# Layer 2's state step: GpSimd adds both halves of a step's output in one operation of 1024 columns

## The chip, the cores and the metric

The kernel runs on one core of one Trainium2 chip. The core has five engines that run side by side: TensorE (PE, matrix products, with its weight loads as PEld), VectorE (DVE), ScalarE (ACT), GpSimd (POOL) and SyncE (SP, here mostly an issuer of DMAs). They wait for one another through semaphores. The metric is the time of one execution on the device in microseconds (us), lower is better; the number given is the median of several runs.

## What is computed

Four layers in a row; each is `x = x + s * silu(f)`, with a sequence mixer s and a mixture of experts f, both of the normalised x. The change lies in layer 2, whose mixer is a selective scan over 512 places for four batches, 256 channels and 16 states:

```python
def step(h, inp):
    dt_t, B_t, C_t, x_t = inp
    h = jnp.exp(dt_t[..., None] * A) * h + dt_t[..., None] * B_t[:, None, :] * x_t[..., None]
    y = jnp.einsum('ben,bn->be', h, C_t)
    return (h, y)
...
y = (y + x_main * D_param) * jax.nn.silu(z)
y = jnp.einsum('ble,de->bld', y, W_out)
out = y + residual
```

Its mixture has 8 experts with 512 hidden units each, of which every token takes two. Each is computed for all tokens and weighed.

## The kernel before

Channels lie on the 128 partitions in two halves m, places along the columns, so one tile of a batch is 128 x 2 x 512, that is 1024 columns. The 16 states are taken one after the other. So layer 2 is a loop of 64 steps k (4 batches b, 16 states n), written out by hand for each engine, and the order in which an engine's code stands is the order in which it works. A step k on the engines:

- ScalarE, `decays(k)` (L2270): the decay factors of a state, into `DA` (`wide` in the trace).
- TensorE, `b_row` and `c_row` (L2102, L2108, in the trace L410, banks<-BCR,SEL): spreads B's and C's row of the state over all partitions, into a PSUM bank.
- VectorE, `inputs(k)` (L2423): DTX times B's row, into `H[:, k % 4]`, one of four buffers; `scan(k)` (L2430): the recurrence along the columns, both halves in one operation with decays and inputs as operands, both in SBUF; `outs(k)` (L2438): H times C's row, two operations of 512 columns, each of which counts the semaphore `hc` up by one.
- GpSimd, `add_y(k)` (L1985): adds H to the running sum `YY`, two operations of 512 columns. For the first state of a batch the sum starts from `XD`, the D term.

VectorE's loop is software-pipelined: in step k it issues scan(k), outs(k-1), inputs(k+2) and, in even steps, `add_expert` (L2454), four operations that add an expert's output for the four tiles of tokens. inputs(k+2) overwrites the buffer of step k-2, so it waits until `ya`, which counts GpSimd's adds, says that add_y(k-2) is done. Between these, at set values of n, stand each batch's other parts: the next batch's normalisation (`stats_in`), router (`take_logits`, `choose`, with L2381), step sizes (`correction`, `dt_sums` with L2408, `dt_x`) and the last batch's end (`gated` L2461, which waits for all 32 adds of its batch, `take_out`, `out_stats`, `finish`).

GpSimd's loop is: add_y(k-1), then at n = 2 the norm's `scales` for the next batch (L381, L382, L1964, L1965, small operations), at n = 4 `out_scales` (L381, L382, L1972, L1973), and in the last batch `early_scales` for layer 3. It works through them in order.

TensorE runs the experts between the rows of B and C: `hidden` (banks<-XT,we) and `chunk` (banks<-we,HH), and in steps 4 to 10 of a batch the projections for the next one. c_row(k) waits for both halves of outs(k-1), since there is one bank for C's row.

Of the kernel before, what the change touches and what calls it, by code (L numbers as in the profile page):

```python
# [20 lines left out]
ALU = mybir.AluOpType  # L21
# [12 lines left out]
def build(nc, I, out):  # L34
    ctx = ExitStack()
    with ctx:
# [3 lines left out]
        def sbr(name, shape, dt=F32, c=None):  # L40
            return sb(name, shape, dt, c, "right")
# [4 lines left out]
        def linker(eng, chain):  # L46

            n = [0]

            def link(ins):  # L50
                n[0] += 1
                ins.then_inc(chain, 1)
                eng.wait_ge(chain, n[0])
            return link
# [324 lines left out]
        def norm_pool(plink, var, rs):  # L379

            plink(nc.gpsimd.tensor_scalar(rs, var, EPS, None, ALU.add))  # L381
            return nc.gpsimd.tensor_tensor(rs, rs, neg_half[:, 0:rs.shape[1]], ALU.pow)  # L382
# [32 lines left out]
        def lsem(name):  # L415
            h = scope[0].enter_context(nc.semaphore(name))
            lsems.append(h)
            return h
# [1449 lines left out]
        def layer2(fcT, pjT, feats, wide, XM, mv3, rstd3):  # L1868
# [6 lines left out]
            bm, ex, scn, hc, ya, yi = (lsem(f"a2_{k}") for k in ("inputs", "decays", "scans", "outs", "y", "y_begun"))  # L1875
# [26 lines left out]
            for k in range(NK):  # L1902
                b, n = divmod(k, NS)
# [19 lines left out]
            with ExitStack() as c:  # L1923
                DTX = sbr("DTX", [P, 2, 2, S], c=c)
                H = sbr("H", [P, 4, 2, S], c=c)
                YY = sbr("YY", [P, 2, S], c=c)
# [15 lines left out]
                XD = [SA4[:, 3, :, :].rearrange(flat), SA[:, :, :].rearrange(flat)]  # L1942
# [7 lines left out]
                with nc.Block() as block:  # L1950
                    @block.sync
                    def _(sp):
                        sp.dma_start(wrow, bcast(I["L2_attn_conv_w"].rearrange("e a k -> (e a k)"), 768)).then_inc(wr, 16)

                    @block.gpsimd
                    def _(g):
                        plink = linker(g, pl)

                        def scales(b):
                            g.wait_ge(var, b + 1)  # L1960
                            if b:
                                g.wait_ge(xn, T * b)
                            plink(norm_pool(plink, mv[:, :, 1], rstd[:, :]))
                            plink(nc.gpsimd.tensor_tensor(shift[:, :], mv[:, :, 0], rstd[:, :], ALU.mult))  # L1964
                            nc.gpsimd.tensor_scalar(shift[:, :], shift[:, :], -1.0, None, ALU.mult).then_inc(rs, 1)  # L1965

                        def out_scales(b):
                            g.wait_ge(var2, b + 1)
                            if b:
                                g.wait_ge(xo2, T * b)  # L1970
                            plink(norm_pool(plink, mv2[:, :, 1], rstd2[:, :]))
                            plink(nc.gpsimd.tensor_tensor(shift2[:, :], mv2[:, :, 0], rstd2[:, :], ALU.mult))  # L1972
                            nc.gpsimd.tensor_scalar(shift2[:, :], shift2[:, :], -1.0, None, ALU.mult).then_inc(rs2, 1)  # L1973

                        def add_y(k):
                            b, n = divmod(k, NS)
                            if n == 0 and b:
                                g.wait_ge(yz, b)
                            for m in range(2):
                                if n == 0:  # L1980
                                    g.wait_ge(yi, 2 * b + m + 1)
                                else:
                                    g.wait_ge(ya, 2 * k + m - 1)
                                g.wait_ge(hc, 2 * k + m + 1)
                                nc.gpsimd.tensor_tensor(YY[:, m, :], YY[:, m, :] if n else XD[m], H[:, k % 4, m, :],  # L1985
                                                        ALU.add).then_inc(ya, 1)

                        def early_scales(b):
                            ts = slice(b * T, (b + 1) * T)
                            g.wait_ge(nv, b + 1)  # L1990
                            if b:
                                g.wait_ge(nx, T * b)
                            else:
                                g.wait_ge(xn, T * B)
                            plink(norm_pool(plink, mv3[:, ts, 1], rstd3[:, ts]))
                            plink(nc.gpsimd.tensor_tensor(shift[:, :], mv3[:, ts, 0], rstd3[:, ts], ALU.mult))
                            nc.gpsimd.tensor_scalar(shift[:, :], shift[:, :], -1.0, None, ALU.mult).then_inc(nr, 1)

                        nc.gpsimd.memset(XT[:, :, 0:1], 0.0)
                        nc.gpsimd.memset(XT[:, :, S + 1:S + 2], 0.0).then_inc(zd, 1)  # L2000
                        nc.gpsimd.memset(BCR[0:32, :, :].bitcast(F32), 0.0).then_inc(zd, 1)
                        scales(0)
                        g.wait_ge(wj, 2)
                        nc.gpsimd.memset(DA[:, :, 1, 0:1], 0.0).then_inc(zd, 1)
                        for k in range(1, NK):
                            b, n = divmod(k, NS)
                            add_y(k - 1)
                            if n == 2 and b + 1 < B:
                                scales(b + 1)
                            if n == 4 and b:  # L2010
                                out_scales(b - 1)
                            if b == B - 1 and n in (2, 5, 8):
                                early_scales((2, 5, 8).index(n))
                        add_y(LAST)
                        out_scales(B - 1)

# [1253 lines left out]
```

## Time and profile before

| | |
|---|---|
| median of 3 runs | 1391.28 us (1389.5 to 1394.29) |
| the profiled execution | 1392.78 us, its span 1391.0 us |
| busy: TensorE / its weight loads | 1151.0 (83%) / 811.3 us (58%) |
| busy: VectorE | 999.5 us (72%) |
| busy: ScalarE | 763.7 us (55%) |
| busy: GpSimd | 614.8 us (44%) |
| layer 2's steps | some 758 to 1184 us of the span |

The span runs from the first instruction of the program to the last; the rest of an execution's time lies around it. A row of a timeline gives start, length, engine, line, operation, the tiles that it writes and reads, their shape, and in brackets how long the engine sat idle before it and who ended that; x4 means that four like instructions were merged to one row. Where a line is a helper's (L410 is every product), the tiles tell which it is. The chain of work that ended last, as the page gives it, covers only the last part of the program and says nothing on layer 2; a stage is read by its window.

### The profile page before, as it was taken

The page shows a single profiled execution, that of the slowest core. Times are in us where ns is not written, and L with a number is a line of the kernel's source. Part 1 is how long each engine was busy: PE and PEld are TensorE (multiplying, and loading weights), DVE is VectorE, ACT ScalarE, POOL GpSimd, SP SyncE. Part 2 cuts the span into 40 slices and gives each one's busy share as a digit, 9 for nine tenths or more (in the row PEclk, how much of TensorE's full clock was granted, in tenths as well). Part 3 has the DMA queues.
Part 4 walks back from the last instruction along what each step waited for, and adds up shares of the span by engine and source line. Part 5 has one row for each costly group of instructions (what it writes and reads, how often), then busy time and mean ns, then how long its engine had stood idle before and what let it go on. Part 6 is the DMA issues. An engine that isn't in the chain of part 4 may idle for free. (4 is left out here: it accounts for less than half of the span.)

```text
span 1391.0 us, 21029 instructions
## 1 busy us (share of the span) xinstructions
PE 1151.0 (83%) x7010; PEld 811.3 (58%) x7010; DVE 999.5 (72%) x2280; ACT 763.7 (55%) x1586; POOL 614.8 (44%) x607
## 2 busy tenths in 40 slices
PE   3999999999898879367766888888888977889995
PEld 1455665665465568156653655655645655668885
DVE  2466767678787727277765989989998999535555
ACT  1456556555544527144446867667768675345552
POOL 4243445444336834554100533733643565216672
PEclk9999999999999989589987999999899889799997
DMA  7400000000000023550000000000000000101113
GB/s 176 121 1 1 1 1 1 1 1 1 1 5 22 28 63 116 154 163 16 1 13 0 1 1 1 1 1 1 1 1 1 1 1 0 31 10 40 43 44 107
DMA packets 54443, 40.71 MB, mean 29 GB/s; under 512 B 13185, under 2 KB 46687, under 8 KB 54337
## 3 DMA queue, kind: packets, MB, share of 16 engines
q1 hardware_dynamic: 40994, 27.58, 6.8%
q0 software_dynamic: 4544, 9.32, 2.4%
q10 hardware_dynamic: 8800, 2.48, 0.9%
q8 instruction: 58, 0.95, 0.3%
q14 instruction: 47, 0.39, 0.1%
HBM read 26.32 MB, written 13.04 MB: 28 GB/s over the span
## 5 line engine op out<-in xcount | busy, mean ns | idle before, releaser
L780 POOL TENSOR_TENSOR PR<-PR,R 128x512 f32<-128x512 f32 (+3 forms) x128 | 160.3, 1264 | 233.1 <-DVE R L1275 232.5
L1985 POOL TENSOR_TENSOR YY<-YY,H 128x512 f32<-128x512 f32 x120 | 164.1, 1390 | 182.0 <-DVE H L2438 182.0
L410 PE MATMUL banks<-XT,we 128*128 128x128 f32 (+1 forms) x568 | 175.8, 442 | 14.0 <-ACT HH L2258 13.7
L1074 ACT ACTIVATE PR<-banks,NM 128x257 f32<-128x257 f32 (+3 forms) x256 | 132.2, 526 | 94.7 <-DVE NM L1247 93.0
L410 PEld LDWEIGHTS banks<-we,HH 128*128 128x128 f32 x1024 | 144.9, 205 | 35.7 <-issue 31.2
L2430 DVE TENSOR_TENSOR_SCAN H<-wide,H 128x1024 f32<-128x1024 f32 x64 | 164.1, 2564 | 0.2
L410 PE MATMUL banks<-we,HH 128*128 128x128 f32 x1024 | 145.1, 288 | 0.0
L410 PEld LDWEIGHTS banks<-XT,we 128*128 128x128 f32 x568 | 89.5, 201 | 65.5 <-issue 41.2
L2258 ACT ACTIVATE HH<-banks,be1f 128x512 f32<-128x512 f32 x128 | 83.4, 685 | 73.7 <-PE banks L410 72.8
L410 PE MATMUL banks<-BCR,SEL 96*128 96x512 f32 x128 | 67.1, 526 | 63.8 <-DVE H L2438 55.4
L410 PEld LDWEIGHTS banks<-PTS,V 128*64 128x64 f32 x1152 | 65.7, 138 | 83.4 <-issue 48.5
L410 PE MATMUL banks<-PTS,V 128*64 128x128 f32 (+1 forms) x1152 | 93.1, 296 | 24.1 <-issue 11.0
L1247 DVE TENSOR_REDUCE NM<-banks 128x2 f32<-128x514 f32 (+3 forms) x128 | 102.7, 823 | 3.3
L1256 DVE COPY PTS<-banks 128x384 f32<-128x384 f32 (+1 forms) x96 | 57.5, 599 | 60.7 <-PE banks L936 59.8
L410 PE MATMUL banks<-KT,QT 64*128 64x384 f32 (+3 forms) x512 | 96.2, 474 | 1.5 <-issue 0.8
L936 PE MATMUL banks<-ident,PR 128*128 128x128 f32 x640 | 92.5, 285 | 2.1 <-POOL PR L780 1.8
L936 PEld LDWEIGHTS banks<-ident,PR 128*128 128x128 f32 x640 | 73.4, 145 | 31.6 <-issue 31.6
L2438 DVE TENSOR_TENSOR H<-H,banks 128x512 f32<-128x512 f32 x128 | 80.8, 671 | 7.5 <-PE banks L410 7.5
L2270 ACT ACTIVATE wide<-feats,Aneg 128x512 f32<-128x512 f32 (+1 forms) x128 | 81.9, 710 | 0.4
L2423 DVE TENSOR_TENSOR H<-DTX,banks 128x1024 f32<-128x1024 f32 x64 | 77.5, 1212 | 1.1 <-PE banks L410 0.9
L410 PEld LDWEIGHTS banks<-BCR,SEL 96*128 96x128 f32 x128 | 26.3, 206 | 72.0 <-DVE H L2438 61.9
L2747 POOL DMA_INDIRECT XS<-xrows,GIX x39 | 38.3, 982 | 53.5 <-DVE GIX L3157 37.3
(568 smaller groups left out, 2445.9 us busy)
## 6 DMA issues: line engine op xcount, KB each, us to landing
xsort<-zrow SPq DMA_DIRECT2D x1, 3072.0 KB, 13.6
XS<-xsort SPq DMA_DIRECT2D x12, 256.0 KB, 2.9
ysort<-PTS SPq DMA_DIRECT2D x12, 256.0 KB, 2.2
pj_stage<-in_L_ffn_w_proj SPq DMA_DIRECT2D x1, 2048.0 KB, 11.9
we<-in_L_ffn_we SPq DMA_DIRECT2D x1, 2048.0 KB, 15.3
we<-yrows SPq DMA_DIRECT2D x8, 256.0 KB, 5.4
xrows<-XN SPq DMA_DIRECT2D x4, 256.0 KB, 3.4
out<-XN SPq DMA_DIRECT2D x4, 256.0 KB, 2.3
```

The source lines that it names most:

```text
L410: return nc.tensor.matmul(o, l, r, start=start, stop=stop)
L780: last = nc.gpsimd.tensor_tensor(p, p, R[:, T * q + t, :].unsqueeze(2).to_broadcast([P, 2, w]), ALU.mult)
L936: last = nc.tensor.transpose(PS[:, 4 + s, k * P:(k + 1) * P], PR0[:, q % 2, s, a:a + P], ident[:, :])
L1074: nc.scalar.activation(PR0[:, q % 2, s, OFF[t]:OFF[t] + w], ps2(n)[:, s, SLOT[t]:SLOT[t] + w], ACT.Exp, bias=NM[:, m, s:s + 1], accum_out= ...
L1247: last = nc.vector.tensor_reduce(NM[:, T * q + t, :], ps2(n)[:, :, SLOT[t]:SLOT[t] + (t + 1) * P + more], AX.X, ALU.max, negate=True)
L1256: nc.vector.tensor_copy(PTS[:, m % 2, 1, 0:w], PS[:, 5, 0:w]).then_inc(ptB, 1)
L1985: nc.gpsimd.tensor_tensor(YY[:, m, :], YY[:, m, :] if n else XD[m], H[:, k % 4, m, :], ALU.add).then_inc(ya, 1)
L2258: nc.scalar.activation(HH[:, i, :], PS[:, 3 + g % 3, :], ACT.Silu, bias=be1f[:, j % NE, i:i + 1]).then_inc(hs, 1)
L2270: nc.scalar.activation(DA[:, k % 4, m, m:], DT[:, b % 2, m, m:], ACT.Exp, scale=Aneg[:, m, n:n + 1]).then_inc(ex, 1)
L2423: nc.vector.tensor_tensor(H[:, k % 4, :, :], DTX[:, b % 2, :, :], PS[:, 1, :].unsqueeze(1).to_broadcast([P, 2, S]), ALU.mult).then_inc(bm, 1)
L2430: nc.vector.tensor_tensor_scan(h, DA[:, k % 4, :, :].rearrange("p m s -> p (m s)"), h, 0.0, ALU.mult, ALU.add).then_inc(scn, 1)
L2438: nc.vector.tensor_tensor(h, h, PS[:, 2, :], ALU.mult).then_inc(hc, 1)
```

## The change

`add_y` issues one operation over both halves, 1024 columns, for every state but a batch's first. It waits for both halves of the step's output and for the whole add before it, and counts `ya` up by two, so that all who wait for `ya` see the same values. The first state keeps its two operations, since `XD`'s halves lie in different tiles.

```diff
--- before.py
+++ after.py
@@ -1976,14 +1976,15 @@
                             b, n = divmod(k, NS)
                             if n == 0 and b:
                                 g.wait_ge(yz, b)
-                            for m in range(2):
-                                if n == 0:
+                            if n:
+                                g.wait_ge(ya, 2 * k)
+                                g.wait_ge(hc, 2 * k + 2)
+                                nc.gpsimd.tensor_tensor(YY[:, :, :], YY[:, :, :], H[:, k % 4, :, :], ALU.add).then_inc(ya, 2)
+                            else:
+                                for m in range(2):
                                     g.wait_ge(yi, 2 * b + m + 1)
-                                else:
-                                    g.wait_ge(ya, 2 * k + m - 1)
-                                g.wait_ge(hc, 2 * k + m + 1)
-                                nc.gpsimd.tensor_tensor(YY[:, m, :], YY[:, m, :] if n else XD[m], H[:, k % 4, m, :],
-                                                        ALU.add).then_inc(ya, 1)
+                                    g.wait_ge(hc, 2 * k + m + 1)
+                                    nc.gpsimd.tensor_tensor(YY[:, m, :], XD[m], H[:, k % 4, m, :], ALU.add).then_inc(ya, 1)
 
                         def early_scales(b):
                             ts = slice(b * T, (b + 1) * T)
```

Only GpSimd's instructions change (the line after the batch's first add has moved with the code). On GpSimd, at the beginning of layer 2, before the change, with the semaphores that each instruction waits for (`a2_outs` is `hc`, `a2_y` is `ya`, `a2_y_begun` tells that XD is there):

```order
L1985 TENSOR_TENSOR YY<-SA_117,H 128x512 [waits a2_outs,a2_y_begun]
L1985 TENSOR_TENSOR YY<-SA,H 128x512 [waits a2_outs,a2_y_begun]
L1985 TENSOR_TENSOR YY<-YY,H 128x512 [waits a2_outs,a2_y] x2
L381 TENSOR_SCALAR rstd<-mv 128x4 [waits a2_xn,a2_var]
L382 TENSOR_TENSOR rstd<-rstd,neg_half 128x4 [waits a2_pool_steps]
L1964 TENSOR_TENSOR shiftb<-mv,rstd 128x4 [waits a2_pool_steps]
L1965 TENSOR_SCALAR shiftb<-shiftb 128x4 [waits a2_pool_steps]
L1985 TENSOR_TENSOR YY<-YY,H 128x512 [waits a2_outs,a2_y] x28
```

The same place with the change:

```order
L1987 TENSOR_TENSOR YY<-SA_117,H 128x512 [waits a2_outs,a2_y_begun]
L1987 TENSOR_TENSOR YY<-SA,H 128x512 [waits a2_outs,a2_y_begun]
L1982 TENSOR_TENSOR YY<-YY,H 128x1024 [waits a2_outs,a2_y]
L381 TENSOR_SCALAR rstd<-mv 128x4 [waits a2_xn,a2_var]
L382 TENSOR_TENSOR rstd<-rstd,neg_half 128x4 [waits a2_pool_steps]
L1964 TENSOR_TENSOR shiftb<-mv,rstd 128x4 [waits a2_pool_steps]
L1965 TENSOR_SCALAR shiftb<-shiftb 128x4 [waits a2_pool_steps]
L1982 TENSOR_TENSOR YY<-YY,H 128x1024 [waits a2_outs,a2_y] x14
```

Two adds of 512 columns have become one of 1024 wherever YY is added to itself; the small operations of the norm keep their place between the first and the second such add of a batch.

## Rows read from the trace of the kernel before

**Rows 1.** Busy time by engine in layer 2's window; columns named above it.

```profile
core 0: us, PE busy (x) PEld busy (x) DVE busy (x) ACT busy (x) POOL busy (x), PEclk, DMA share, GB/s
758.00:1184.00 426.00, 354.58 (x1650) 243.53 (x1651) 402.73 (x576) 298.37 (x419) 206.04 (x164) 0.91 0.00 1
```

**Rows 2.** Costliest groups: operation xcount | busy us, mean ns | idle before, releaser.

```profile
L1985 POOL TENSOR_TENSOR YY<-YY,H 128x512 f32<-128x512 f32 x120 | 164.1, 1390 | 182.0 <-DVE H L2438 182.0
...
L2430 DVE TENSOR_TENSOR_SCAN H<-wide,H 128x1024 f32<-128x1024 f32 x64 | 164.1, 2564 | 0.2
...
L2438 DVE TENSOR_TENSOR H<-H,banks 128x512 f32<-128x512 f32 x128 | 80.8, 671 | 7.5 <-PE banks L410 7.5
```

**Rows 3.** Single lines: duration in ns, min/median/max, first and last start.

```profile
L2430 DVE TENSOR_TENSOR_SCAN H<-wide,H x64: 2256/2288/3231, 758.3 to 1170.6; 128x1024 f32<-128x1024 f32 x64
...
L1985 POOL TENSOR_TENSOR YY<-YY,H x120: 1257/1276/3262, 772.0 to 1178.2; 128x512 f32<-128x512 f32 x120
...
L2408 DVE TENSOR_TENSOR feats<-feats,DTX x4: 1225/2080/2089, 748.8 to 1063.3; 128x1024 f32<-128x1024 f32 x4
...
L2381 DVE TENSOR_TENSOR PR<-LG,rt x4: 192/836/839, 756.3 to 1022.1; 128x32 f32<-128x32 f32 x4
```

**Rows 4.** VectorE's timeline, first long scan, then steps 25 and 26.

```profile
766.89 3.16 DVE L2430 TENSOR_TENSOR_SCAN H<-wide,H 128x1024 f32<-128x1024 f32 x1
...
919.22 1.11 DVE L2454 SCALAR_TENSOR_TENSOR ACC<-banks,WG,ACC 128x128 f32<-128x128 f32 x4
920.25 2.28 DVE L2430 TENSOR_TENSOR_SCAN H<-wide,H 128x1024 f32<-128x1024 f32 x1
922.96 1.28 DVE L2438 TENSOR_TENSOR H<-H,banks 128x512 f32<-128x512 f32 x2 [0.42 <-PE banks L410]
924.16 1.22 DVE L2423 TENSOR_TENSOR H<-DTX,banks 128x1024 f32<-128x1024 f32 x1
925.29 3.16 DVE L2430 TENSOR_TENSOR_SCAN H<-wide,H 128x1024 f32<-128x1024 f32 x1
```

**Rows 5.** VectorE's timeline at the end of the last batch.

```profile
1170.60 3.23 DVE L2430 TENSOR_TENSOR_SCAN H<-wide,H 128x1024 f32<-128x1024 f32 x1
...
1179.61 1.23 DVE L2461 TENSOR_TENSOR SA<-SA,YY 128x1024 f32<-128x1024 f32 x1 [1.69 <-POOL YY L1985]
```

**Rows 6.** VectorE's timeline, the scan of step 4.

```profile
780.25 2.92 DVE L2430 TENSOR_TENSOR_SCAN H<-wide,H 128x1024 f32<-128x1024 f32 x1
```

**Rows 7.** GpSimd's timeline beside rows 4, steps 25 and 26.

```profile
917.72 2.51 POOL L1985 TENSOR_TENSOR YY<-YY,H 128x512 f32<-128x512 f32 x2 [4.83 <-DVE H L2438]
923.79 2.52 POOL L1985 TENSOR_TENSOR YY<-YY,H 128x512 f32<-128x512 f32 x2 [3.56 <-DVE H L2438]
```

**Rows 8.** GpSimd's timeline beside rows 6, the two adds in windows of their own.

```profile
779.74 1.28 POOL L1985 TENSOR_TENSOR YY<-YY,H 128x512 f32<-128x512 f32 x1
...
780.98 3.25 POOL L1985 TENSOR_TENSOR YY<-YY,H 128x512 f32<-128x512 f32 x1
```

**Rows 9.** GpSimd's groups by shape: the multiply of layer 0.

```profile
L780 POOL TENSOR_TENSOR PR<-PR,R 128x1024 f32<-128x1024 f32 x32 | 60.7, 1897 | 44.9 <-DVE R L1275 44.8
...
L780 POOL TENSOR_TENSOR PR<-PR,R 128x512 f32<-128x512 f32 x32 | 33.8, 1055 | 57.4 <-DVE R L1275 56.9
```

**Rows 10.** GpSimd's timeline at the end of the last batch.

```profile
1174.56 4.95 POOL L1985 TENSOR_TENSOR YY<-YY,H 128x512 f32<-128x512 f32 x4 [2.87 <-DVE H L2438]
```

**Rows 11.** Who waited for whom, VectorE, 757 to 1185 us: total, times, longest.

```profile
DVE H L2438 <- PE banks L410: 7.5, 6, 3.2
DVE PR L2387 <- ACT PR L2226: 7.1, 3, 2.7
...
DVE SA L2461 <- POOL YY L1985: 1.7, 1, 1.7
```

**Rows 12.** VectorE's timeline in the second batch.

```profile
938.75 1.29 DVE L2438 TENSOR_TENSOR H<-H,banks 128x512 f32<-128x512 f32 x2 [3.17 <-PE banks L410]
```

**Rows 13.** TensorE's timeline: its waits for VectorE around rows 12.

```profile
910.90 0.53 PE L410 MATMUL banks<-BCR,SEL 96*128 96x512 f32 x1 [2.78 <-DVE H L2438]
...
949.05 0.50 PE L410 MATMUL banks<-BCR,SEL 96*128 96x512 f32 x1 [2.11 <-DVE H L2438]
```

## The prediction, made before the changed kernel was run

> **What bounds the kernel now.** I read the window of layer 2's state steps first, then the groups of instructions, then the timelines of VectorE and GpSimd side by side, and last who waits for whom. The change touches the window from 758 to 1184 us alone. There VectorE is busy 402.7 of 426 us (95%), TensorE 354.6 (83%), GpSimd 206 (48%) [rows 1]. So VectorE sets the pace, and GpSimd, on which the changed operation runs, has time to spare: 120 adds of 128x512, 164.1 us in all, and 182.0 us of waiting for VectorE before them [rows 2]. Shorter adds are worth nothing by themselves. What matters is what an add does to VectorE.
>
> It does something. The scan, the costliest of VectorE's operations here, takes 2.26 us at least, 2.29 in the median and 3.23 at most [rows 3], 2.56 on the mean of 64 [rows 2]. In the timeline 41 scans take 2.26 to 2.32 us, 15 take 3.14 to 3.23 (766.89 is the first, 1170.60 the last [rows 4, 5]) and 8 take 2.90 to 2.94 (the first is at 780.25 [rows 6]): 15 x 0.87 + 8 x 0.64 = 18.2 us over the floor of 2.28, which is also 64 x 0.284. Three patterns explain all of them.
>
> Long hit: two adds run from 923.79 to 926.31; the scan starts at 925.29, 1.02 us before they end, and takes 3.16 instead of 2.28 us [rows 4, 7]. It pays the overlap less 0.13 us. Near miss: the adds end at 920.23, the scan starts at 920.25 and takes 2.28; here four expert additions (1.11 us from 919.22) stand between the outputs and the scan [rows 4, 7]. Thirteen scans are such, all behind a step with expert additions. Split hit: where GpSimd comes late from its small norm operations, the first add runs 779.74 to 781.02; the scan, started at 780.25, gets in behind that add and takes 2.92; the second add, started at 780.98, then takes 3.25 us [rows 6, 8]. So an add and a scan exclude each other, and the second of the two waits until the first one's instruction ends. VectorE's operations that read one operand from a PSUM bank do not stretch: the two outputs beside an add take 1.28 us together, the input 1.22 [rows 4].
>
> The Trainium skill (SBUF — State Buffer, "Who interferes with whom") has this rule: a VectorE instruction with two SBUF inputs and a GpSimd instruction that reads SBUF hold the shared port for a whole instruction each, and whoever is first blocks the other. It speaks against this change: a longer add is a longer hold. If instead a hold could be passed on within an instruction, the third term of the sum below would be gone, and the sum would be 7 us lower. The trace agrees with the rule as far as single adds go, but for the 0.13 us.
>
> **The change part by part.** It removes 60 of 120 adds and has 60 of 1024 columns; the first add of each of the four batches stays in two halves. SyncE, TensorE, ScalarE and VectorE get the same instructions in the same order.
>
> Length of the new add. The trace has no such add of 1024 columns. Nearest is GpSimd's multiply PR: 1.055 us for 512 columns and 1.897 for 1024 [rows 9], so 1.645 ns a column and 0.21 us fixed. An add of 512 takes 1.257 us at least [rows 3]; with the same fixed part it is 2.04 ns a column, and 1024 columns take 0.21 + 2.09 = 2.30 us. Bounds: 1.90 us (the multiply's) and 2.51 (two adds as now). I take 2.30, as the 512-column adds stand nearest.
>
> By the Trainium skill (GPSIMD Engine Reference, "3.1 Elementwise — side-by-side cycle accounting") an add of 2048 columns takes 4.497 us. With the trace's 1.257 for 512 that makes, as an estimate, 2.34 for 1024, and the sum 1 us higher.
>
> When it ends. The wait is now for both halves of the output. A pair of halves takes 1.25 to 1.28 us, with its second started shortly before the first has ended [rows 4], and one half 0.67 on the mean [rows 2], so the second is ready 0.59 us after the first. The add starts 0.59 later and ends at +0.59 + 2.30 - 2.51 = +0.38 us against now. Behind a late GpSimd it starts as now, and ends 2.30 instead of 1.28 us after its start, +1.02 as far as the next scan is concerned.
>
> The sum on VectorE:
> - Long hits: 15, of which four follow a batch's first add, which stays as it is. 11 x 0.38 = 4.2 us.
> - Near misses: 13 x (0.38 - 0.02 - 0.13) = 3.0 us.
> - Split hits: 8, of which 7 have a half add before the scan and another behind it (in the eighth both halves were done before it). 7 x 1.02 = 7.1 us.
> - Other operations with two SBUF inputs that are hit now in the same way: three of L2408 (2.08 instead of 1.23) and three of L2381 (0.84 instead of 0.19) [rows 3]. 6 x 0.38 = 2.3 us.
> - The end: VectorE waits 1.69 us for the last adds before the gate [rows 5]. They run 1174.56 to 1179.51 [rows 10]; now they would start at 1175.15 and take 2 x 2.30, to 1179.75: +0.2 us.
>
> Together 16.8 us. Nothing comes off: the time that GpSimd saves, 60 x 0.2 us, is idle time. The reuse of the four buffers of H is not at stake. The step that refills a buffer waits for an add two steps back, and VectorE has no wait for GpSimd in this window other than the one at the end [rows 11].
>
> What hides part of it. VectorE waits 7.5 us for TensorE at its output line and 7.1 us for ScalarE [rows 11], nearly all of it before the last steps. In each of the first three batches the projections for the next one make TensorE the late one: between 910.90 and 949.05 it waits for no output of VectorE, and VectorE waits 3.17 us for it at 938.75 [rows 12, 13]. What VectorE loses in between costs nothing: one L2381, one near miss and one long hit, 0.38 + 0.23 + 0.38 = 1.0 us a batch, 3.0 in three. Further short waits take another 1 to 2 us. If this cover is gone, all of 16.8 counts; if the cover reaches back further, through TensorE's own slack, it can take at most some 14 us. I take 4.4 off: **+12.4 us**. The profiled execution took 1392.8 us and would take 1405.2; the median of the runs is 1.5 us lower (0.1%), so 1391.3 + 12.4 = 1403.7.
>
> **Rivals.**
> The add is cheap or the loss is covered (0.12). If 1024 columns take 1.90 us, adds end 0.02 us earlier than now; long hits and near misses stay, split hits cost 7 x 0.62 = 4.3 and the end gives 0.6 back: about +3 us, 1394. If TensorE's stretches cover nearly the whole sum, it is 1392 to 1395 too. For it: the multiply's row. Against it: 1.257 us for 512 columns, and that VectorE is 95% busy.
>
> The scan wins the race (0.04), the case on the other side. Were the add to start behind the scan, it and not the scan would wait, as the second add does at 780.98, with slack behind it. All 18.2 us of stretched scans would go; at the same cover that is about 13 us, 1378. It decides at an add that starts later than its scan: the start moves by 0.59 us, and 923.79 + 0.59 = 924.38 is still 0.91 before 925.29.
>
> Dearer (0.14). An add of 1024 columns takes 2.51 us and nothing is covered: 11 x 0.59 + 7 x 1.23 + 13 x 0.44 + 6 x 0.59 + 0.7 = 25 us, 1416. For it: VectorE's share of 95%. Against it: that two starts become one.
>
> That the change does not do what it says is out: the program has 60 adds of 1024 columns on GpSimd.
>
> **How the numbers follow.** The forecast, +7 to +17 us, has 0.70. The range takes in the cover from none to double and the length from 2.1 to 2.4 us: 1396 to 1412. A difference of 0.3% (4.2 us) is about what a measurement can tell from no change: faster 0.04 (the race), same 0.12 (cheap or covered), slower 0.84 (forecast and dearer).
>
> **What would show it.** The new add at 2.3 us. Scans: no longer some 41 undisturbed but about 28, 13 of them now near 2.5 us, 11 near 3.5 and 7 near 3.9; mean from 2.56 to about 2.79 us. VectorE's waits for TensorE and ScalarE in the window a few us shorter, L2408 near 2.46. The window itself 12 us longer, and the rest of the program unchanged. I am wrong if the scans' mean stays at 2.56 (then the port is not held for the instruction), or if it rises and the window doesn't grow (then the cover is larger than I think).

## The result and the profile after

The change made the kernel slower: 1408.82 us as the median of 4 runs (1405.79 to 1411.74) against 1390.39 us of the kernel before (4 runs), a ratio of 1.0127 with a 95% interval of 1.0105 to 1.0148, that is 14.6 to 20.6 us, 17.7 in the middle. The forecast was 12.4 us, and 1403.7 us. The profiled execution took 1408.26 us with a span of 1406.5.

The groups of the page, for the two lines that [rows 2] show before the change (operation xcount | busy us, mean ns | idle before, releaser):

```profile
L1982 POOL TENSOR_TENSOR YY<-YY,H 128x1024 f32<-128x1024 f32 x60 | 141.8, 2364 | 223.0 <-DVE H L2439 222.9
...
L2431 DVE TENSOR_TENSOR_SCAN H<-wide,H 128x1024 f32<-128x1024 f32 x64 | 182.0, 2844 | 0.2
```

GpSimd's adds went from 164.1 to 141.8 us, 22 us less for an engine that had time anyway. The scans, on which nothing was changed, went from 164.1 to 182.0 us, 18 us more for the engine that has none. Single lines, duration in ns as min/median/max (compare [rows 3]):

```profile
L2431 DVE TENSOR_TENSOR_SCAN H<-wide,H x64: 2257/2602/4002, 756.7 to 1182.4; 128x1024 f32<-128x1024 f32 x64
...
L1982 POOL TENSOR_TENSOR YY<-YY,H x60: 2347/2364/2378, 771.1 to 1190.0; 128x1024 f32<-128x1024 f32 x60
...
L2409 DVE TENSOR_TENSOR feats<-feats,DTX x4: 1224/2560/2566, 747.3 to 1069.9; 128x1024 f32<-128x1024 f32 x4
...
L2382 DVE TENSOR_TENSOR PR<-LG,rt x4: 191/1316/1320, 754.8 to 1028.0; 128x32 f32<-128x32 f32 x4
```

The floor of the scan has not moved, but its median has, from 2.29 to 2.60 us, and its maximum from 3.23 to 4.00. VectorE's timeline at steps 25 and 26, and GpSimd's beside it, the places of [rows 4, 7]:

```profile
924.07 2.60 DVE L2431 TENSOR_TENSOR_SCAN H<-wide,H 128x1024 f32<-128x1024 f32 x1
926.59 1.25 DVE L2439 TENSOR_TENSOR H<-H,banks 128x512 f32<-128x512 f32 x2
927.77 1.21 DVE L2424 TENSOR_TENSOR H<-DTX,banks 128x1024 f32<-128x1024 f32 x1
928.90 3.63 DVE L2431 TENSOR_TENSOR_SCAN H<-wide,H 128x1024 f32<-128x1024 f32 x1
```

```profile
922.15 2.37 POOL L1982 TENSOR_TENSOR YY<-YY,H 128x1024 f32<-128x1024 f32 x1 [5.46 <-DVE H L2439]
928.01 2.36 POOL L1982 TENSOR_TENSOR YY<-YY,H 128x1024 f32<-128x1024 f32 x1 [3.49 <-DVE H L2439]
```

The first add ends at 924.52, 0.45 us after its scan began; that scan, a near miss before, takes 0.32 us more than its floor. The second ends 1.47 us into the scan, which takes 1.35 more. In both the scan pays the overlap less 0.12 or 0.13 us. And where GpSimd comes late, in step 4 (compare [rows 6, 8]), VectorE and GpSimd:

```profile
778.69 3.99 DVE L2431 TENSOR_TENSOR_SCAN H<-wide,H 128x1024 f32<-128x1024 f32 x1
```

```profile
778.18 2.35 POOL L1982 TENSOR_TENSOR YY<-YY,H 128x1024 f32<-128x1024 f32 x1
```

No add ends at 0.77 us after the scan's start any more, to let it in; it waits for the whole add, to 780.53.

Where the time went is seen best from the first scan's start to the last one's. The two stretches, before and after (columns: us, then busy us of PE, PEld, DVE, ACT, POOL, and TensorE's granted clock):

```profile
758.29:1170.60 412.31, 345.70 (x1601) 236.12 (x1601) 392.66 (x561) 294.63 (x412) 200.00 (x160) 0.91 0.00 1
```

```profile
756.74:1182.43 425.69, 356.10 (x1601) 245.42 (x1602) 413.50 (x562) 294.71 (x412) 177.46 (x102) 0.88 0.00 1
```

VectorE is busy for 20.8 us more. Its idle time, the stretch less the busy time, fell from 19.7 to 12.2 us. The difference, 13.4 us, is what the stretch grew by. So some 7.5 us of the loss were hidden in time in which VectorE had waited for others before. VectorE's waits, to be read against [rows 11], and the place of [rows 12]:

```profile
DVE PR L2388 <- ACT PR L2227: 4.9, 3, 1.7
DVE H L2439 <- PE banks L410: 2.9, 4, 0.8
```

```profile
940.33 1.28 DVE L2439 TENSOR_TENSOR H<-H,banks 128x512 f32<-128x512 f32 x2 [0.79 <-PE banks L410]
```

The wait of 3.17 us is down to 0.79, those for ScalarE from 7.1 to 4.9 in all. The end of the layer, the places of [rows 5, 10]:

```profile
1192.45 1.22 DVE L2462 TENSOR_TENSOR SA<-SA,YY 128x1024 f32<-128x1024 f32 x1 [2.20 <-POOL YY L1982]
```

```profile
1187.50 4.84 POOL L1982 TENSOR_TENSOR YY<-YY,H 128x1024 f32<-128x1024 f32 x2 [3.50 <-DVE H L2439]
```

VectorE waits 2.20 us there, not 1.69.

### The profile page after: what moved, and what is told of

Its sections match the earlier page's. It is cut to its first block and busy times, and to the rows that moved or that the text cites. A ratio compares the mean times of both kernels' runs of the same rounds, so it can differ in the third digit from the quotient of the medians.

```text
span 1406.5 us, 20909 instructions
## 1 busy us (share of the span) xinstructions
PE 1163.5 (83%) x7010; PEld 823.9 (59%) x7010; DVE 1020.5 (73%) x2280; ACT 764.2 (54%) x1586; POOL 592.7 (42%) x547
## 5 line engine op out<-in xcount | busy, mean ns | idle before, releaser
L1982 POOL TENSOR_TENSOR YY<-YY,H 128x1024 f32<-128x1024 f32 x60 | 141.8, 2364 | 223.0 <-DVE H L2439 222.9
L2431 DVE TENSOR_TENSOR_SCAN H<-wide,H 128x1024 f32<-128x1024 f32 x64 | 182.0, 2844 | 0.2
L410 PEld LDWEIGHTS banks<-we,HH 128*128 128x128 f32 x1024 | 152.9, 215 | 36.3 <-issue 31.0
L410 PE MATMUL banks<-we,HH 128*128 128x128 f32 x1024 | 152.8, 298 | 0.0
L410 PE MATMUL banks<-BCR,SEL 96*128 96x512 f32 x128 | 71.0, 557 | 69.2 <-DVE H L2439 60.8
```

The costliest lines, as they stand in the source:

```text
L410: return nc.tensor.matmul(o, l, r, start=start, stop=stop)
L1982: nc.gpsimd.tensor_tensor(YY[:, :, :], YY[:, :, :], H[:, k % 4, :, :], ALU.add).then_inc(ya, 2)
L2431: nc.vector.tensor_tensor_scan(h, DA[:, k % 4, :, :].rearrange("p m s -> p (m s)"), h, 0.0, ALU.mult, ALU.add).then_inc(scn, 1)
```

## The experiments

Three questions: is it the exclusion of the two engines that costs the time, is it the end or the length of an add that counts, and can the stretch that was there before the change be had back? The kernels were timed against the kernel before on the same chip. This table holds the ratio, and the stretch from the first scan to the last in the profiled execution, with VectorE's busy time in it and the rest (us). Where the text gives a kernel's difference in us, it is the ratio's; the medians give up to 2 us less or more. The stretch is that of one execution, which can lie some us beside its kernel's median (1379.41 for 1382.5 us in fitted_four, 1380.5 for 1384.89 in fitted):

| kernel | ratio (95% interval) | stretch | busy | idle |
|---|---|---|---|---|
| before | | 412.3 | 392.7 | 19.7 |
| changed | 1.0127 (1.0105 to 1.0148) | 425.7 | 413.5 | 12.2 |
| late_halves | 0.9991 (0.9976 to 1.0006) | 414.2 | 393.2 | 21.0 |
| no_read | 0.9866 (0.9849 to 0.9882) | 397.5 | 375.1 | 22.4 |
| five_buffers | 0.9982 (0.9969 to 0.9995) | 412.3 | 392.7 | 19.6 |
| behind_scan | 1.0084 (1.0067 to 1.0101) | 423.4 | 395.5 | 27.9 |
| merge_late | 1.0023 (1.0006 to 1.0039) | 417.1 | 399.7 | 17.4 |
| merge_rest | 1.0046 (1.0025 to 1.0067) | 417.6 | 405.3 | 12.3 |
| quarters | 0.9993 (0.9980 to 1.0006) | 411.7 | 385.5 | 26.2 |
| quarters_five | 1.0002 (0.9986 to 1.0017) | 410.8 | 387.0 | 23.8 |
| eighths | 1.0068 (1.0052 to 1.0084) | 415.4 | 383.1 | 32.3 |
| fitted | 0.9955 (0.9939 to 0.9972) | 402.6 | 382.4 | 20.2 |
| fitted_four | 0.9942 (0.9924 to 0.9961) | 402.5 | 382.5 | 20.0 |
| fitted_late | 0.9961 (0.9945 to 0.9978) | 405.0 | 378.3 | 26.7 |

**no_read: GpSimd as busy, but without reading.** From the changed kernel:

```diff
-nc.gpsimd.tensor_tensor(YY[:, :, :], YY[:, :, :], H[:, k % 4, :, :], ALU.add).then_inc(ya, 2)
+plink(nc.gpsimd.memset(YY[:, :, :], 0.0))
+plink(nc.gpsimd.memset(YY[:, :, :], 0.0))
+nc.gpsimd.memset(YY[:, 0, :], 0.0).then_inc(ya, 2)
```

> The changed kernel, but the add of 1024 columns is replaced by three memsets of the sum tile (1024, 1024 and 512 columns, some 2.5 us together), with the same waits and counts; the sums over the states are left out. GpSimd is as busy, but reads nothing from SBUF. Theory (the two engines exclude each other where both read SBUF, VectorE with two operands): all scans but the few beside the small norm operations and the four first adds fall to 2.28 us, and the time is 10 to 20 us under the kernel before. Rival (GpSimd's late end or its semaphores hold VectorE up): the time stays with the changed kernel, 15 us or more over the kernel before.

1375.31 us against 1392.17, 18.7 us under the kernel before by the ratio (16.9 by the medians). The scan's line:

```profile
L2433 DVE TENSOR_TENSOR_SCAN H<-wide,H x64: 2256/2284/3193, 757.7 to 1155.2; 128x1024 f32<-128x1024 f32 x64
```

```profile
757.73:1155.23 397.50, 341.26 (x1600) 235.61 (x1601) 375.14 (x562) 294.73 (x412) 180.16 (x216) 0.92 0.00 1
```

Only four scans are over 2.3 us, at 3.16 to 3.19, those behind each batch's first adds, which were left as they are. GpSimd is as busy as in the changed kernel (180 us to 177) and its waits and counts are the same. So neither its load nor its semaphores make the scans longer; its reading does. That settles the first question, for the scans. It does not hold for every operation: a cast that starts with the last memset of a step takes 0.80 us, where the same cast takes 0.42 us in the kernel before, with no add beside it. VectorE and GpSimd in no_read:

```profile
818.49 0.80 DVE L2397 CAST BCR<-XNT 32x512 fp32r<-32x512 f32 x1
```

```profile
818.49 0.52 POOL L1984 MEMSET YY<- 128x512 f32 x1
```

**late_halves: the later start, without the merging.** From the kernel before:

```diff
-g.wait_ge(hc, 2 * k + m + 1)
+g.wait_ge(hc, 2 * k + (2 if n else m + 1))
```

> Two adds of 512 columns as before the change, but both wait for the second half of the step's output. Theory (an add and a scan exclude each other, so what counts is when the adds end): the pair starts 0.59 us later and ends 0.59 us later; the long scans grow from 3.16 to about 3.7 us, the near misses from 2.28 to about 2.7, but the scans of 2.90 us stay, since the scan can still get in between two adds. VectorE loses about 16 us against the kernel before, where the changed kernel loses about 21; at the same cover the time is 10 to 14 us over the kernel before. Rival (it is the length of the one operation that hurts, not its end): within 3 us of the kernel before. Rival (the later release of the sum or of H's buffers stalls VectorE): VectorE shows waits for GpSimd before its input operation.

My theory gave +10 to 14 us, and the kernel is as fast as the one before. What it had left out is in the timelines of VectorE and, in a window of its own, of GpSimd's first add of the step:

```profile
917.76 2.71 DVE L2430 TENSOR_TENSOR_SCAN H<-wide,H 128x1024 f32<-128x1024 f32 x1
...
922.70 2.52 DVE L2430 TENSOR_TENSOR_SCAN H<-wide,H 128x1024 f32<-128x1024 f32 x1
```

```profile
921.79 1.29 POOL L1985 TENSOR_TENSOR YY<-YY,H 128x512 f32<-128x512 f32 x1 [3.47 <-DVE H L2438]
```

The scan at 922.70 waits only for the add that is in flight, to 923.08, and takes 2.52 us; the other add comes behind it. Long hits fall from 3.16 to 2.52, near misses rise from 2.28 to 2.61 or 2.71: 11 x 0.63 us down against 14 x 0.33 to 0.43 up (the prediction counted 13 near misses, the traces have 14), and 0.3 up for two more, about even. What I had called a split hit is the general case. The price of an add is not when the step's work ends but how much of one instruction is left when the scan arrives. So the later start costs nothing as long as there is a boundary between the two halves; without it, it does. Where the merged add starts no later than the pair did, behind a GpSimd that is late, and the scan used to come in the second half, the scan even gets shorter. That is step 54, before and after the change:

```profile
1117.17 2.94 DVE L2430 TENSOR_TENSOR_SCAN H<-wide,H 128x1024 f32<-128x1024 f32 x1
```

```profile
1126.27 2.81 DVE L2431 TENSOR_TENSOR_SCAN H<-wide,H 128x1024 f32<-128x1024 f32 x1
```

In the plain steps the loss takes both, the later start and the missing boundary, and the change can't have the one without the other, as its add needs both halves of the output.

**merge_late and merge_rest: the terms of the sum apart.** The merged add in 9 of the 60 steps, behind GpSimd's small norm operations, and in the other 51:

```diff
-if n:
+if k in (2, 18, 20, 34, 36, 50, 52, 53, 56):
...
```

The dots stand for the rest of the edit: the other steps keep their two adds. merge_rest has `if n and k not in` these steps.

> The change in 9 of 60 steps alone: those whose add comes behind GpSimd's small norm operations (the steps whose scans are split hits, and two that follow them). Theory: 7 scans go from 2.9 to 4.0 us, little else changes, VectorE loses 7.6 us and at a cover of a third the time is 4 to 7 us over the kernel before. Rival (every merged add costs the same): 9/60 of 17.7, 2.7 us.

> The change in the other 51 steps. Theory: 11 scans of 3.62 us (3.15 before), 13 near misses of 2.60 (2.28 before), the split hits stay at 2.91; VectorE loses about 13 us, and the time is 8 to 12 us over the kernel before. Rival (every merged add costs the same): 51/60 of 17.7, 15 us.

merge_late has seven scans of 3.99 to 4.00 us and VectorE's busy time is 7.0 us longer, for nine merged adds; merge_rest has 12.7 us for fifty-one. Together 19.7 of the changed kernel's 20.8. So the merged adds don't all cost the same on VectorE, 0.78 us each behind the norm operations and 0.25 elsewhere. The times, 3.2 and 6.4 us over the kernel before, lie below both expectations (4 to 7 and 8 to 12); of the rivals, 15 us for merge_rest is out, but 2.7 us for merge_late is not, as its interval is 0.8 to 5.4 us. The two times add up to 9.6 us and not to 17.7. Each alone uses the same idle time as cover (2.2 and 7.4 us of it, where both together had 7.5), but that is only some 3 us of the gap: the two stretches grew by 4.8 and 5.3 us, the changed kernel's by 13.4. The rest is open (see the end of the next section).

**five_buffers and behind_scan: the reuse of H, and a start behind the scan.** `H` with five buffers; in behind_scan also the merged add behind `g.wait_ge(scn, k + 3)`, and the norm operations ahead of it.

> The kernel before with five buffers for H in place of four (the scaled convolution weights move to a tile that is free in this layer); an input operation then waits for an add one step older. Theory: no wait for a buffer exists, so the time is that of the kernel before within 2 us. Rival (adds that end late hold up the reuse of H): faster by 3 us or more.

> The changed kernel with five buffers for H, and each add (but a batch's last) waits until the scan after next has ended, so that it runs beside the outputs and inputs, which read one operand from PSUM; GpSimd's small norm operations go ahead of the add. Theory: an add of 2.36 us that starts 0.14 us behind a scan's end overlaps the next scan by about 0.25 us in plain steps and not at all in steps with expert additions; scans in plain steps take about 2.4 us, those beside late norm operations 3 to 4 us. The stretch of all scans falls from 18 us (36 in the changed kernel) to 8 to 12, and the time is 3 to 10 us under the kernel before. Rival (the length of the operation hurts wherever it lies): the time stays 10 us or more over the kernel before.

Five buffers leave the stretch at 412.3 us to a tenth: the buffers aren't at stake (the ratio, 0.9982, says 2.5 us faster, just outside the 2 us expected; nothing in layer 2 stands for it). behind_scan does what it should to the plain scans, about 2.4 us each. But the add now lies beside other operations with two SBUF inputs. In step 12 the correction is hit, VectorE and GpSimd:

```profile
836.54 3.25 DVE L2405 TENSOR_TENSOR DTX<-EW,DTX 128x1024 f32<-128x1024 f32 x1
```

```profile
836.06 2.65 POOL L1984 TENSOR_TENSOR YY<-YY,H 128x1024 f32<-128x1024 f32 x1 [8.89 <-DVE H L2433]
```

and scans 17, 33 and 49, behind two adds in a row, take 3.9 us, those behind late norm operations 4.0. VectorE ends up 2.9 us busier than before the change, and idle for 8.2 us more, in waits for TensorE. Why TensorE is later there I have not settled. The expectation, 3 to 10 us faster, was wrong; the kernel is 11.7 us slower.

**quarters, eighths and quarters_five: smaller pieces.** Each half in two pieces (the edit shown) or, in eighths, in four, only the last of which counts `ya` up:

```diff
+for p in range(2):
+    cs = slice(p * (S // 2), (p + 1) * (S // 2))
+    last = nc.gpsimd.tensor_tensor(YY[:, m, cs], ..., H[:, k % 4, m, cs], ALU.add)
+last.then_inc(ya, 1)
```

> The kernel before with four adds of 256 columns a step in place of two of 512; each pair waits for its half of the output. Theory (a scan waits for the one add that is in flight, and the rest of the pieces come behind the scan): a piece takes about 0.73 us, so a scan waits 0.6 us at most and 0.25 on the mean; GpSimd is busier, 2.9 us a step. The scans' stretch falls from 18.2 us to 8 to 11, near misses are hit by some 0.2 us; the time is 3 to 8 us under the kernel before. Rival (what counts is when the last add of a step ends): 0.4 us later for each plain step, 5 to 12 us over the kernel before.

> The kernel before with eight adds of 128 columns a step. Theory: a piece takes about 0.47 us, eight of them 3.8 us, and a scan waits 0.35 us at most; stretch of the scans 4 to 9 us, and the time 4 to 11 us under the kernel before, if GpSimd, at 3.8 us of a step's 6.5 plus the time it is held up, doesn't become the late one. Rival (end of the last add): 10 us or more over the kernel before.

> Four adds of 256 columns a step with five buffers for H. With four buffers VectorE waited 0.85 us four times for GpSimd. Theory: these 3.4 us go, the scans' stretch stays near 10 us, and the time is 2 to 5 us under the kernel before. Rival (TensorE holds the gain): within 2 us of the kernel with four buffers.

The theory holds on VectorE: pieces take 0.73 and 0.45 us, and its busy time falls by 7.2 and 9.6 us. It gives nothing back in time: quarters and quarters_five are as fast as the kernel before, eighths is 9.5 us slower. In quarters the idle time rises by nearly as much, in eighths by more, since eight adds of 0.45 us are 3.6 us a step where two took 2.5, and VectorE now waits for GpSimd (VectorE's waits of these two, total, times, longest):

```profile
DVE H L2441 <- PE banks L410: 11.5, 7, 4.2
...
DVE H L2426 <- POOL YY L1987: 3.4, 4, 0.9
```

```profile
DVE H L2426 <- POOL YY L1987: 9.1, 14, 1.3
```

Here H's buffers do matter. With a fifth one the waits of 3.4 us are gone, but the stretch is only 0.9 us shorter, and the time the same. The rival was right that VectorE waits the gain away, most of it for TensorE. That this must be so is not shown. Below stand the third batch's steps 0 to 11, with the next batch's projections in them, in quarters and in fitted_four, one of the kernels of the next experiment (columns as above):

```profile
969.18:1053.00 83.82, 72.43 (x330) 49.81 (x330) 74.61 (x121) 55.96 (x81) 51.73 (x58) 0.90 0.00 1
```

```profile
962.73:1043.72 80.99, 69.90 (x332) 47.79 (x332) 74.47 (x122) 55.99 (x81) 49.02 (x40) 0.94 0.00 1
```

VectorE is busy for the same time, and quarters takes 2.8 us longer, with TensorE's granted clock at 0.90 and not 0.94. In the second batch it takes 81.72 us for 80.24, with the clock at 0.96 against 0.94. So the clock is a rival for one part and not for the other, and no run here separates it from the order in which the engines meet.

**fitted, fitted_four, fitted_late: the boundary where the scan arrives.** Only one half of an add is cut, so that an instruction ends when a scan is due:

```diff
+if k in (2, 18, 20, 34, 36, 50, 56):
+    cuts = (0, 128, S) if m == 0 else (0, S)
+elif k % 2 == 0 or k == 61:
+    cuts = (0, S) if m == 0 else (0, 128, S)
+else:
+    cuts = (0, S)
...
```

The dots stand for the loop that issues one add for each piece.

fitted has five buffers, fitted_four the four of before, and fitted_late has 256 in place of 128 in the first line of cuts.

> The kernel before with five buffers for H, and with one half of a step's add cut into 128 and 384 columns where the traces show a scan arriving: the second half in even steps, the first half in the seven steps behind GpSimd's small norm operations. So an instruction ends 0.1 to 0.2 us after, or just before, the scan is due. Theory (the scan waits for the end of the instruction in flight, less 0.13 us): long hits wait 0.1 us in place of 0.87, split hits 0 to 0.1 in place of 0.64; the scans' stretch falls from 18.2 us to 2 to 5, that of all VectorE operations from 22.6 to about 7. Without waits for H the window loses 8 to 13 us, and the time is 6 to 12 us under the kernel before. Rival (TensorE is the next bound and takes the gain back, as in the kernels with small pieces): within 3 us of the kernel before.

> As the kernel with fitted cuts, but with the four buffers of H. Theory: in the seven steps behind the small norm operations nearly all of an add now comes behind the scan, and the input operation waits some 1 us for it: 5 to 7 us of VectorE's waits for GpSimd, and the time 3 to 6 us over the kernel with five buffers. Rival (buffers don't matter): the same time.

> As the kernel with fitted cuts and four buffers, but in the seven steps behind GpSimd's small norm operations the first half is cut into 256 and 256 columns, not 128 and 384. Theory (the scan waits for the end of the instruction in flight, less 0.13 us): that scan arrives 0.51 us after the add's start, when 128 columns (0.45 us) have just ended and the 384 behind them are in flight; a piece of 256 (0.73 us) ends 0.22 us after the scan is due, so the scan takes 2.37 us in place of 3.05. VectorE's stretch falls by another 4.8 us, and the time is 2 to 5 us lower, 9 to 13 us under the kernel before. Rival (TensorE or the wait for H's buffers takes it back): no lower than with 128 and 384.

fitted_four has the lowest ratio of those that compute everything: 1382.5 us against 1391.28, 0.9942, about 8 us under the kernel before and some 26 under the changed one. fitted is 6.3 us under the kernel before; the intervals of the three overlap. Its scan of step 26, and that of step 4:

```profile
919.92 2.35 DVE L2438 TENSOR_TENSOR_SCAN H<-wide,H 128x1024 f32<-128x1024 f32 x1
```

```profile
777.78 3.05 DVE L2438 TENSOR_TENSOR_SCAN H<-wide,H 128x1024 f32<-128x1024 f32 x1
```

All fifteen long hits are down to 2.33 to 2.46 us. The seven split hits got worse, 3.05 for 2.91: the piece of 128 columns was over before the scan came, and the scan met the 384 behind it. VectorE is busy for 10.2 us less than in the kernel before and the stretch is 9.8 us shorter, so here, other than in quarters, nearly all of the gain comes through. The fifth buffer did nothing, against my expectation of 5 to 7 us of waits. fitted_late cures the seven scans, 2.38 us as worked out:

```profile
782.26 2.38 DVE L2438 TENSOR_TENSOR_SCAN H<-wide,H 128x1024 f32<-128x1024 f32 x1
```

VectorE is 4.1 us less busy than in fitted_four, and idle for 6.7 us more, 2.9 of them waits for H's buffers and most of the rest for TensorE. So it is no faster, 5.4 us under the kernel before where I expected 9 to 13; its interval and that of fitted_four overlap.

## Why the prediction came out as it did

The direction, the mechanism and nearly all places were right, and 1408.8 us lies in the range of 1396 to 1412; the forecast of +12.4 us was 5 us low, 2 us under the interval. The prediction gives its 0.70 to +7 to +17 us, which isn't quite the same range: 17.7 us lies just above it.

- *Length of the new add*: 2.30 us forecast, 2.36 measured. The estimate of 2.34 by the figure for 2048 columns in the Trainium skill (GPSIMD Engine Reference, "3.1 Elementwise — side-by-side cycle accounting") was nearer. The start moved by 0.62 us and not by 0.59. So the end moved by 0.48 us and not by 0.38, and that is in each term of a plain step.
- *Long hits*: 11 x 0.47 = 5.2 us (4.2 forecast). *Near misses*: there are 14, not 13 (the prediction missed one), 14 x 0.33 = 4.6 (3.0). *Split hits*: 7 x 1.08 = 7.6 (7.1). *Other operations*: 6 x 0.48 = 2.9 (2.3).
- *Not in the sum*: the scans of steps 5 and 59, from 2.32 to 2.61 us. They stand behind a split hit. The add beside them ended 0.17 us behind the scan's start, now 0.46. And three casts and two multiplies of other parts, about 0.5 us for each kind. Together some 1.6 us. Step 54, which the prediction has as done with both halves before its scan (its second add was in flight), gave 0.1 back.
- *The end*: +0.5 us (0.2 forecast), 2.20 us of waiting for 1.69, which is no busy time.
- So some 22 us on VectorE, where the sum had 16.8. *The cover* was mis-sized the other way: 7.5 us of idle time vanished, 4.4 forecast. I had counted only what VectorE lost between TensorE's last wait for it and its own wait for TensorE; the waits at 827.34, 832.45, 938.75 and 1050.59 us of the trace before took more than that, 6.1 us. That the two errors took away most of each other, +14 us where +12.4 stood, is luck.
- Between the profiled executions lie 15.5 us. 13.4 are in the stretch of the scans and 0.5 in each of the last scan and the wait behind it; the rest comes before and after. From the last scan's end to the end of the span the kernels of this study took 215 to 221 us (eighths 225), so 2 us more or less there tell nothing.
- *The rivals*: "cheap" fell with 2.36 us for an add. "The scan wins the race" did not happen in the changed kernel, but it is what each boundary between two adds allows, and the fitted kernels got 5 to 8 us by it. I had taken it for a matter of start times, and not seen that the kernel before had such a boundary in every step.

By the Trainium skill (SBUF — State Buffer, "Who interferes with whom") the shared port is held for a whole instruction. Single adds, merged adds and pieces all agree here, with the waiting scan let in at the first boundary, 0.13 us before the overlap's end as the records have it.

Open: TensorE's granted clock in the stretch was 0.88 in the changed kernel's profiled execution, 0.91 before and 0.90 to 0.93 in the others. Over the whole execution it was 0.904 to 0.912 in all four executions of the changed kernel, and 0.917 to 0.927 in those of the kernel before that the experiments were timed against; merge_late and merge_rest have 0.921 and 0.926 on the mean. Executions of one kernel with a lower clock are mostly the longer ones (fitted_four: 1379.41 us at 0.929, 1385.13 at 0.923). The scans' lengths need no clock: each follows from the add beside it. And VectorE's idle time for TensorE fell all the same. But it may have a part in the 3 us of the 17.7 that the sum doesn't reach, and in the gap between 9.6 us for the two parts of the change and 17.7 for the whole. No run separates it.

## What to carry to other kernels

Before two GpSimd operations are merged, look at what VectorE does beside them: where both read SBUF and VectorE reads two operands from it, the boundary between two instructions is where VectorE gets in, and one long instruction takes it away. A gain on an engine that has time to spare is worth nothing, and its instructions' length can be a cost on the one that has none; cut them so that one ends when the other engine arrives, and no finer. And a loss or gain on the bounding engine is worth only what is left after the stretches in which another engine is late: here two thirds of a loss came through, of the gains by small pieces nothing, and of the gain by fitted pieces nearly all, so it has to be measured each time.

## What the runs showed of the hardware that I had not expected

- Of two adds that stand one behind the other on GpSimd with their waits met, the second does not keep a waiting scan out: the scan starts at the boundary each time (2.52 us for a scan 0.38 us before the first add's end, 4.51 us for the pair).
- GpSimd's add takes some 0.45, 0.73, 1.27 and 2.36 us for 128, 256, 512 and 1024 columns of float32 in two SBUF operands.
- Three memsets in a row, some 2.5 us of GpSimd a step, cost VectorE's scans nothing. But a cast of 32x512 beside a memset takes 0.80 us in place of 0.42.
